# 16-head attention: TensorE's products with V and its transposes change places in each step

## The reference, cut to what matters

```
q = (hidden_states @ Wq.T).reshape(B, S, NUM_HEADS, HEAD_DIM).transpose(0, 2, 1, 3)
scores = jnp.einsum('bhqd,bhkd->bhqk', q, k) * scale + causal
probs = jax.nn.softmax(scores, axis=-1)
out = jnp.einsum('bhqk,bhkd->bhqd', probs, v)
return out.transpose(0, 2, 1, 3).reshape(B, S, NUM_HEADS * HEAD_DIM) @ Wo.T
```

```
S_shifted = jnp.roll(S, 1, axis=-2).at[:, 0, :].set(0.0)
FF = jnp.cumsum(S_shifted, axis=-2)
att = att - FF[:, None]
sorted_idx = jnp.argsort(FF_mod, axis=-1)        # the smallest FF are kept
y = jax.nn.softmax(jnp.where(keep[:, None], att, neg_inf), axis=-1) @ v
```

## Time and profile before

| what | value |
|---|---|
| median of 3 runs | 4163.04 us (4160.76 to 4163.07) |
| the profiled execution's own time | 4161.85 us |
| its span, first to last instruction | 4160.3 us |
| mean granted TensorE clock | 0.869 of full speed |
| PE busy | 3228.8 us, 78% |
| DVE busy | 2775.4 us, 67% |
| POOL busy | 1637.5 us, 39% |
| ACT busy | 1405.4 us, 34% |
| A1 in the first batch, S(0) to the start of L619 | 146.97 to 226.12 us |
| A2 in the first batch, S(0) to the start of L619 | 288.10 to 410.76 us |

### The profile page before, as it was taken

One profiled execution on the slowest core, in us unless ns is written; L12 is line 12 of the kernel. 1 busy time (PEld: TensorE's weight loads), 2 busy tenths in 40 slices (PEclk: granted clock), 3 DMA queues, 4 the chain that ended last, 5 costly groups with the idle time before them and its releaser, 6 DMA issues. The chain is left out here.

```text
span 4160.3 us, 46406 instructions
## 1 busy us (share of the span) xinstructions
PE 3228.8 (78%) x17780; PEld 2134.8 (51%) x17780; DVE 2775.4 (67%) x4417; ACT 1405.4 (34%) x2256; POOL 1637.5 (39%) x972
## 2 busy tenths in 40 slices
PE   4877967778787797877868679688787867877787
PEld 2434446665353445666525344567743544366673
DVE  2457379996255638999515662999941575399993
ACT  1434223333253423333325332333332533233332
POOL 0212067772031207777103120877700311177770
PEclk9988978889898897888989789788898979888998
DMA  3000100000100010000000001000000000100001
GB/s 115 1 1 1 48 6 1 1 1 21 34 1 1 1 53 1 1 1 1 26 29 1 1 1 53 1 1 1 1 26 29 1 1 8 46 1 1 1 1 28
DMA packets 62136, 56.52 MB, mean 14 GB/s; under 512 B 6171, under 2 KB 47539, under 8 KB 61766
## 3 DMA queue, kind: packets, MB, share of 16 engines
q1 hardware_dynamic: 52800, 44.62, 3.5%
q10 hardware_dynamic: 9094, 8.72, 0.7%
HBM read 52.28 MB, written 1.05 MB: 13 GB/s over the span
## 5 line engine op out<-in xcount | busy, mean ns | idle before, releaser
L1255 POOL TENSOR_TENSOR arena<-arena 128x2048 f32<-128x2048 f32 (+7 forms) x384 | 1320.6, 3472 | 446.1 <-DVE arena L1304 351.2
L1174 PE MATMUL psum<-ident,arena 128*128 128x128 f32 (+7 forms) x9216 | 1153.6, 290 | 402.9 <-DVE arena L1304 290.3
L1174 PEld LDWEIGHTS psum<-ident,arena 128*128 128x128 f32 (+7 forms) x9216 | 1094.3, 145 | 505.4 <-DVE arena L1304 312.4
L1239 ACT ACTIVATE arena<-arena 128x2048 f32<-128x2048 f32 (+2 forms) x320 | 530.2, 1662 | 958.3 <-DVE arena L1291 958.2
L1304 DVE TENSOR_TENSOR arena<-arena,psum 128x2048 f32<-128x2048 f32 (+7 forms) x384 | 631.2, 1658 | 13.8 <-PE psum L1174 13.8
L1291 DVE TENSOR_TENSOR arena<-arena,psum 128x2048 f32<-128x2048 f32 (+7 forms) x384 | 631.3, 1659 | 4.4 <-POOL arena L1255 1.8
L743 POOL TENSOR_SCALAR arena<-arena 128x512 f32<-128x512 f32 (+3 forms) x512 | 268.1, 541 | 665.8 <-DVE arena L715 665.8
L462 POOL TENSOR_TENSOR rstd<-veps,mhalf 128x4 f32<-128x4 f32 x32 | 32.4, 1013 | 1209.7 <-DVE veps L453 1209.7
L678 ACT ACTIVATE arena<-arena 128x512 f32<-128x512 f32 (+3 forms) x512 | 281.9, 551 | 358.3 <-DVE arena L710 358.3
L635 PE MATMUL psum<-ident,arena 128*128 128x128 f32 x1280 | 215.5, 314 | 202.1 <-ACT arena L689 124.4
L635 PEld LDWEIGHTS psum<-ident,arena 128*128 128x128 f32 x1280 | 159.9, 156 | 331.1 <-ACT arena L689 188.6
(11 more groups left out here) (208 smaller groups left out, 3610.8 us busy)
## 6 DMA issues: line engine op xcount, KB each, us to landing
stream<-in_L_ffn_W SPq DMA_DIRECT2D x160, 256.0 KB, 3.1
wh<-in_L_ffn_h_w ACTq DMA_DIRECT2D x2, 1024.0 KB
wa<-in_L_attn_W_attn ACTq DMA_DIRECT2D x1, 1536.0 KB
wq<-in_L_attn_Wq ACTq DMA_DIRECT2D x2, 512.0 KB
wo<-in_L_attn_Wo ACTq DMA_DIRECT2D x2, 512.0 KB
x<-in_L_attn_x SPq DMA_DIRECT2D x4, 256.0 KB, 3.7
out_x<-x SPq DMA_DIRECT2D x4, 256.0 KB, 2.3
w<-in_L_ffn_w_w ACTq DMA_DIRECT2D x3, 256.0 KB
```

Of the source, the lines that this page charges most:

```text
L1174: last = nc.tensor.matmul(ps[half][0:rows, f * NH:f * NH + P], buf[:, c:c + rows], ident[:], start=k + j == first_key and f == 0, stop=k + ...
L1239: nc.scalar.activation(D3[n % 5][:, 0:cols], D3[n % 5][:, 0:cols], ACT.Exp).then_inc(s["e"], 1)
L1255: last = nc.gpsimd.tensor_tensor(of_piece(D3[n % 5], piece), q, keys_on(K3[tt % 2], piece), ALU.mult)
```

## The change

In each step of PE, V(t-3) is now issued ahead of T(t-2). Nothing is added or taken away, the waits stay with the instructions they belong to, and the other four engines' lists are the same.

```
                     last.then_inc(s["scores"], 1)
+                if 0 <= t - LO < NG:
+                    heads_values(pe, A, t - LO)
                 if 0 <= t - LX < NG:
                     heads_transpose(pe, A, t - LX)
-                if 0 <= t - LO < NG:
-                    heads_values(pe, A, t - LO)
             pe.wait_ge(s["OT"], NG)
```

## The result

| | before | changed |
|---|---|---|
| median (range) of 6 runs each, same chip | 4161.69 us (4157.07 to 4163.07) | 4196.78 us (4187.24 to 4203.01) |
| ratio, 95% interval | | 1.0083 (1.0068 to 1.0098) |
| the profiled execution's own time | 4161.85 us | 4198.11 us |
| its span | 4160.3 us | 4196.5 us |
| mean granted TensorE clock | 0.869 | 0.870 |

The change made the kernel 35 us slower. The direction was forecast; the size was twice the 17 us that I had worked out, and outside the range.

The account below looks back on a forecast made before the run. DVE was taken to bound A2's pruning, and a chain through S, mask, exp, copy, T and V the rest of A1 and A2. Per batch 0.4 + 1.8 + 2.0 = 4.2 us, 17 us in all: 4180 us, range 4170 to 4192.

Parts of the forecast that it names:

- The reading of the chain: A1's loop through S, mask, exp, copy, T and V keeps its 6.83 us round in either order; cost 0.
- The pruning stretch of A2: While pruning runs in A2, DVE is 95% busy and waits for nothing of PE's; cost 0.
- the heads of the calls: At each call's start, no V can fill T(0)'s wait, and V(0) and T(1) both need copy(0); cost 0.
- The tails: In each call's last steps, V waits for its copy with nothing beside it: +1.8 us in A1, +2.0 in A2.
- The early groups: In A1's early groups, mask(4) comes 0.2 to 0.3 us late; 0.4 us per A1, between 0 and 1.5.
- the sum: Early groups of A1 and both tails added: 4.2 us per batch, 17 us over four batches.
- The clock rival: TensorE's clock falls in the tails, so projections start cold: 4191 for A2's four tails, 4202 for all eight; chance 0.11.
- rule on transposes: Transposes don't engage the full clock, so the tails would lose it, 4191 to 4202; the forecast followed the trace instead.
- The other two rivals: DVE late in every step of A1 (4186, chance 0.06), and loop shortened by an exposed weight load (4172, chance 0.15).
- late in the loop: Rival: DVE 0.2 us late in each of A1's 16 later steps, 6 us more, 4186; chance 0.06.
- the exposed weight load: Rival: T's weight loads run under V's matmuls, 0.15 us off each loop round, 4172; chance 0.15.
- faster by more: Faster by more than 0.2%, needing 0.45 us off every round, more than any gap in rows 3; chance 0.04.

Follow-up runs that it names:

- e6: Changed kernel plus a 700-column dead DVE reduction (about 0.8 us per batch) ahead of norm 5; 4176.89 us, 1.0037 against the kernel before.
- e3: Kernel before, order kept, plus dead DVE reductions ahead of OT(21), about 1.87 us in A1 and 2.08 us in A2; 4189.59 us, 1.0070.
- e1: Kernel before with V ahead of T only in the three steps without scores; 4173.62 us, 1.0029.
- e5: Changed kernel plus a 150-column dead DVE reduction (about 0.24 us per batch) ahead of norm 5; 4188.92 us, 1.0064 against the kernel before.
- e4: Kernel before, order kept, plus one 512-column dead DVE reduction ahead of OT(21) in A1 only; 4162.25 us, 1.0003.
- e10: Kernel before plus a 150-column dead DVE reduction (about 0.24 us per batch) ahead of norm 5; 4163.03 us, 1.0004.
- e7: Kernel before plus a 460-column dead DVE reduction (about 0.55 us per batch) ahead of norm 5; 4148.95 us, 0.9972.

## Why the prediction was wrong

**Right.** The reading of the chain: the round kept its 6.83 us in A1, since V(t-2) needs the very copy that T(t-1) needs. The idle time moved from L635 to L652. The pruning stretch of A2 and the heads of the calls cost nothing (the loop alone 1.0001). The tails cost 1.88 us in A1 (forecast 1.8) and 2.0 in A2 (2.0), with V's two new waits at 0.83 us in A1 and 1.11 in A2. The early groups were mis-sized, 0.17 us for 0.4: mask(4) came 16.14 us behind S(0) before and 16.21 now, 0.07 late and not 0.2 to 0.3, as copy, OT and mask follow each other on DVE at 0.61 and 0.60 us (161.05, 161.66, 162.26 in the changed kernel) and not at the 0.69 that was added up for each. In all the local terms come to some 4.1 us a batch, forecast 4.2.

**The step that failed** is the sum: "Per batch 0.4 + 1.8 + 2.0 = 4.2 us; four batches 17 us", with nothing for what comes behind. It took for granted that a stage whose instructions are unchanged keeps its time when it starts 2 or 4 us later. It doesn't, where PE idles and then feeds an engine that waits for it: 20 of the 36 us stand in what was entered as nothing. The channel stage took between 458.3 and 465.8 us over the twelve kernels and four batches, and it has the same instructions in all of them. The changed kernel's positions happened to be bad (464.7 us in three of four, +10.8 in all), those of the tails alone good (458.4 in three of four, -9.6), and that difference of 20.4 us is most of why +12 and 0 made +35. Both are luck of position: the same change with some 0.8 us more in each batch (e6) measured +16 us, near my 17.

**The clock rival** had the right resource in the wrong place. I put the fall into the tails, for gaps of 1.1 us, at 2.8 us each. There the clock stayed at 1.00; where a projection did meet the low clock, in e3, it cost 1.68 us. It fell in A2 behind a wait of 2.43 us, where it was low for parts of the time in the kernel before too (mean 0.71 over the pruning); only the piece at 1.2 GHz was now another one, on the path: 1.34 us each, 5.4 in all. Not V's wait did that but the position, since e1 has the same loss with T first. The rival's price (4191) would have come near, for a reason that wasn't the true one, and its price for all eight calls (4202) was left outside the range. The range should have held that a shift can change later stages by some us a batch in either direction.

**The Trainium skill's rule on transposes** (page "TensorE: Matmul & The Clock Gate", section "Part 4: PE-mode transpose") that was weighed in the prediction held neither in the tails, where T's transposes are one of the two kinds of block and the clock was 1.00, nor in the channel stage, where L1174 alone runs at full clock once it has risen (changed kernel):

```profile
587.00:591.00 4.00, 4.00 (x39) 1.00 0.00 0
```

**The other two rivals** are out. DVE wasn't late in the loop (+0.17 us an A1 at most), and the exposed weight load brought nothing: the round is the same to 0.01 us. The small chance of "faster by more" rested on the claim that 0.45 us is more than any gap in rows 3; it is more than any gap of PE there (0.41), not of DVE (0.77) or ACT (1.59).

**Shown and open.** Shown: the channel stage's time depends on when it starts relative to the clock's rise (most cleanly in the kernel before with delays of 0, 0.24 and 0.54 us just ahead of it, where both new lengths were expected from the distance before they were measured), and A2 has two lengths with the same instructions. Read afterwards from the traces, with exceptions: which distance gives which time. Open: why those distances give those times, and how to compute the distance of a later batch ahead (in e5 it ranged from 59.14 to 59.56). Open as well is the reason for another thing that the traces show. The distance from one channel stage to the next is 1027.41 us three times in the kernel before, in e4 and in e10, and 1024.00 in e7, and the clock's rise stands equally far behind the start in all four batches of each. Other kernels settle at 1034.24 (e3) and 1030.82 (e6), the changed one has 1037.64 twice. All these lie 3.41 us apart, so a batch seems to lose or gain in steps of that size, and a delay that is too small for a step is given back; a local sum of 4.2 us is no such step. Open, too, is the spread of the changed kernel's runs (4187 to 4203 us, before 4157 to 4163), of which one part may be A2's two lengths, as in e5.

## What to carry to other kernels

Two instructions that wait for the same buffer can't fill each other's wait; look for what stands ahead of the instruction that frees it, in the list of the engine that does so. Here that was worth 62 us (4160.98 to 4099.30), with one block moved on ACT. A software pipeline's order must be read in its tail too, where the block that used to hide a copy is no longer there. And a local sum of a few us carries an error that no local reading shows, as every later stage starts elsewhere under the clock: test a small change beside neutral delays of several sizes before giving its sign or its worth, and check in their traces that the delay itself doesn't bring the clock down, as it did in e3.

## What was not expected of the hardware

- Dead work made a kernel faster: 0.63 us of DVE a batch took 12 us off (0.9972), and a piece of about 0.8 us took 20 us off the changed one.
- The clock's rise doesn't follow the stage: with a start 0.54 us later it came 0.55 us sooner behind the start (58.59 for 59.14), and this distance goes with the stage's length over twelve kernels. The Trainium skill, page "TensorE: Matmul & The Clock Gate", section "Part 1: The HAM clock gate (the "warmup" mystery)", says that the number of slow matmuls at a kernel's start varies from run to run and that for modelling the loss there is under 1% of a typical kernel. No run here measures that start. Further in, the four A2 of one execution (e5) took 124.68, 126.04, 126.00 and 124.68 us. Position was worth -12 us in e7 and is about +20 us in the changed kernel, of 4161; both are under 1%, yet of the size that this whole change was forecast to have (17 us).
- One gap of 2.23 us on PE in front of a projection brought its clock down and cost 1.68 us in it (8.81 us in place of 7.13); three gaps of 1.1 us between blocks of 2.1 us didn't bring it down.
